# Last layer of a two-layer network: MLP, router and expert bias as fp16 halves inside the expert loop

## What is computed

```
# end of the attention-like block, per token
x  = x + o @ Wo
h2 = layernorm(x) * ln_w + ln_b
x  = x + gelu(h2 @ W1 + b1) @ W2 + b2          # "MLP": 128 -> 256 -> 128
# mixture of experts, all 16 experts on all tokens
x_ = layernorm(x)
logits = x_ @ router_w + router_b              # 16 experts
probs  = softmax(logits); top 4, renormalised -> c[token, expert], 0 elsewhere
for e in range(16):
    acc += (gelu(x_ @ w1[e] + b1[e]) @ w2[e] + b2[e]) * c[:, e]     # 128 -> 256 -> 128
out = x + acc
```

## Times and profile before

| | |
|---|---|
| time, median of 3 runs | 1009.13 us (1007.19 to 1015.8) |
| profiled execution, its own time | 1008.39 us |
| its span on the core | 1006.6 us |
| mean granted TensorE clock over the span | 0.919 |
| expert loop, 8 tiles | 619.1 to 1006.6 us |
| PE busy, whole span | 798.5 us |
| DVE busy, whole span | 678.7 us |
| ACT busy, whole span | 621.2 us |
| POOL busy, whole span | 630.4 us |

### The profile page before, as it was taken

The page is one execution under the profiler, slowest core; times in us unless marked ns, Lnnn a source line. Parts: engine busy times, 40 slices in busy tenths (PEclk is TensorE's granted clock), DMA queues, the critical chain, the costliest instruction groups (busy, mean ns, idle before and its releaser), DMA issues.

```text
span 1006.6 us, 17882 instructions
## 1 busy us (share of the span) xinstructions
PE 798.5 (79%) x5918; PEld 479.8 (48%) x5918; DVE 678.7 (67%) x1994; ACT 621.2 (62%) x923; POOL 630.4 (63%) x414
## 2 busy tenths in 40 slices
PE   1976465579777629828767688999999999999997
PEld 0443122125323125613222255777777777777776
DVE  5669899965554357749499776866665656666564
ACT  1755133314332327616967837989898888889895
POOL 4008799610545553646588895777777777777685
PEclk9977899978978858969999987999999999999999
DMA  5899200017000020043150000000000000000000
GB/s 132 99 121 204 91 0 0 17 31 204 31 12 7 4 72 25 23 125 96 45 175 1 0 1 1 2 11 0 10 0 10 0 11 0 10 0 10 0 12 12
DMA packets 52694, 40.42 MB, mean 40 GB/s; under 512 B 5995, under 2 KB 44638, under 8 KB 52638
## 3 DMA queue, kind: packets, MB, share of 16 engines
q1 hardware_dynamic: 49566, 37.27, 17.4%
q0 software_dynamic: 3072, 2.51, 0.9%
HBM read 18.05 MB, written 14.88 MB: 33 GB/s over the span
## 4 chain that ended last, share of the span: by engine, by line
PE 55%; DVE 11%; issue 4%; ACT 3%; another core or an unknown queue 3%; DMA 1%; POOL 1%; DVEq 0%; SPq 0%; POOLq 0%; ACTq 0%
PE PS L1684 53%; DVE scratch L1476 3%; DVE scratch L1484 2%; DVE resid L1413 2%; PE PS L1691 2%; ACT scratch L808 1%; DVE stats L1253 1%; POOL disp L600 1%; DVE scratch L1433 0%; DMA A<-disp 0%; PE PS L2080 0%; DVE scratch L1496 0%; DMA A<-y_rows 0%; DMA disp<-A,scratch 0%
## 5 line engine op out<-in xcount | busy, mean ns | idle before, releaser
L686 POOL TENSOR_TENSOR scratch<-scratch 128x1024 f16<-128x1024 f32 x128 | 272.8, 2133 | 105.2 <-ACT scratch L1065 102.3
L1637 DVE SCALAR_TENSOR_TENSOR resid<-PS,coef,resid 128x128 f32<-128x128 f32 x512 | 144.1, 344 | 135.8 <-PE PS L1684 134.0
L1684 PE MATMUL PS<-A,scratch 128*128 128x128 f16 x3456 | 217.4, 219 | 7.4 <-DVE A L1380 5.2
L1684 PEld LDWEIGHTS PS<-A,scratch 128*128 128x128 f16 x3456 | 204.0, 98 | 40.1 <-DVE A L1380 6.5
L1684 PE MATMUL PS<-A 128*128 (+1 forms) x768 | 188.2, 382 | 0.0
L1061 ACT ACTIVATE scratch<-PS,cols 128x512 f32<-128x512 f32 x256 | 164.0, 684 | 15.6 <-PE PS L1684 14.9
L1065 ACT ACTIVATE scratch<-scratch 128x1024 f16<-128x1024 f32 x128 | 135.3, 1057 | 5.2
L1684 PE MATMUL PS<-scratch,ident 128*128 128x512 f32 x160 | 89.5, 683 | 57.8 <-DVE scratch L1220 56.1
L563 POOL TENSOR_TENSOR scratch<-A 128x1024 f32<-128x1024 f32 x32 | 76.0, 2386 | 84.8 <-DVE A L1194 65.6
L600 POOL DMA_INDIRECT disp<-A,scratch x64 | 65.2, 1018 | 70.1 <-DVE scratch L1316 53.1
L1684 PEld LDWEIGHTS PS<-A 128*128 128x128 f16 x768 | 72.4, 99 | 72.0 <-issue 10.4
(11 more groups left out here) (295 smaller groups left out, 1345.9 us busy)
## 6 DMA issues: line engine op xcount, KB each, us to landing
A<-A SPq DMA_DIRECT2D x22, 256.0 KB, 8.4
y_rows<-zeros SPq DMA_DIRECT2D x8, 512.0 KB, 6.0
A<-y_rows SPq DMA_DIRECT2D x16, 256.0 KB, 3.6
disp<-zeros SPq DMA_DIRECT2D x4, 528.0 KB, 21.7
A<-disp SPq DMA_DIRECT2D x4, 528.0 KB, 5.9
resid<-in_L_attn_x SPq DMA_DIRECT2D x8, 256.0 KB, 4.5
A<-scratch SPq DMA_DIRECT2D x8, 256.0 KB, 7.9
A<-in_L_ffn_ew SPq DMA_DIRECT2D x1, 2048.0 KB, 12.9
```

Source lines behind the costliest of these rows:

```text
L686: pool.tensor_tensor(h_low[n % 4], h_full[n % 2], h_high[n % 4], SUB).then_inc(S("m1_low"), 1)
L1637: last = STT(out=resid[:, g, :], in0=bank(4 + e % 2)[:, t * C:(t + 1) * C], scalar=coef[:, t, e:e + 1], in1=resid[:, g, :], op0=MUL, op1=ADD)
L1684: return nc.tensor.matmul(o, l, r, start=start, stop=stop)
```

## The change

Four products of the side work are now made from fp16 halves: hidden layer and output of the MLP, the router's logits, and the bias times coefficients. For that:

- At the end of the first layer's expert stage ScalarE and VectorE make the halves of W1, W2 and the router's weights, of the identity and of the bias (in three copies, for which there are two more loads).
- VectorE makes the low half of the MLP's input (`hT11_low`, from PSUM), and both halves of the hidden layer (`hid11_split`: a cast and a subtraction for each of two parts). The normalisation's bias moves out of `hT11_copy` into the MLP's bias, with two tiny matmuls early in the program.
- The router takes the halves in `x_hl` that the experts use, so that ScalarE's copy into `xT12` is gone.
- The coefficients are written to one of two buffers; the copy L1674 is gone, and three operations write their scaled halves (`coef_parts`). The transposes of the coefficients are fp16 matmuls by an fp16 identity.
- For experts 5, 8 and 11 (`HIGH_BY_DVE`) VectorE makes `h_high` in place of ScalarE.
- Places: `outputs11` moves from behind e = 5 to behind 6, `add_mlp`, `inverse_deviation` and `normalise12` each one expert later (7, 8, 9), `normalise11` in all tiles to behind 10. `transpose12` stays behind 10.

```diff
-        A_(h_high[e % 4], h_full[e % 2], ACT.Copy).then_inc(S("m1_high"), 1)
+        if e not in HIGH_BY_DVE:
+            A_(h_high[e % 4], h_full[e % 2], ACT.Copy).then_inc(S("m1_high"), 1)
...
+            def hT11_low(c):
+                dve.wait_ge(S("xT_copied"), 3 * B + at(c))
+                STT(out=hT11_hl[:, 1, :], in0=bank(6), scalar=cols[:, LNW1:LNW1 + 1], in1=hT11_hl[:, 0, :], op0=MUL,
+                    op1=SUB).then_inc(S("xT_low"), 1)
+
+            def hid11_split(c, h):
+                dve.wait_ge(S("hid11"), at(2 * c + h))
+                st.done(V.tensor_copy(hid11_high[:, h, :], hid11[:, h, :]))
+                TT(hid11_low[:, h, :], hid11[:, h, :], hid11_high[:, h, :], SUB).then_inc(S("hid11_low"), 1)
+
+            def expert_high(b, e):
+                n = b * E1 + e
+                dve.wait_ge(S("m1_hid"), at(n * HC1 + HC1 - 1))
+                dve.wait_ge(S("m1_out_mm"), at(n, 4))
+                V.tensor_copy(h_high[e % 4], h_full[e % 2]).then_inc(S("eo"), 1)
...
-                st.done(TT(coef_next, weight, over(share_P), MUL))
+                to = coef[c % 2]
+                st.done(TT(to, weight, over(share_P), MUL))
+                high, low, again = (coef_parts[:, :, k * E1:(k + 1) * E1] for k in range(3))
+                TS(again, to, SCALE, None, MUL)
+                st.done(TS(high, to, SCALE, None, MUL))
+                st.done(STT(out=low, in0=to, scalar=SCALE, in1=high, op0=MUL, op1=SUB))
...
             def all_experts(b, next_batch, batch_beyond):
                 for e in range(E1):
+                    if e + 2 in HIGH_BY_DVE:
+                        expert_high(b, e + 2)
                     accumulate(b, e)
...
                     if next_batch:
-                        if e == 6:
+                        if e == 1:
+                            hT11_low(b + 1)
+                        if e == 3:
+                            hid11_split(b + 1, 0)
+                        if e == 5:
+                            hid11_split(b + 1, 1)
+                        if e == 7:
                             add_mlp(b + 1)
...
-                mm(bank(6), tile(u_1, h), hT11).then_inc(S("hid11_mm"), 1)
+                for k, (sw, sx) in enumerate(PARTS):
+                    last = mm(bank(6), tile(u1_hl[:, sw, :], h), hT11_hl[:, sx, :], start=k == 0, stop=k == len(PARTS) - 1)
+                last.then_inc(S("hid11_mm"), 1)
...
-                        if e == 5:
+                        if e == 6:
                             outputs11(b + 1)
```

More of the change, by code:

```diff
@@ L310, in build, with high_made @@
         prob, weight = (sm[:, 128 + 64 * k:192 + 64 * k].rearrange("p (n e) -> p n e", e=E1) for k in range(2))
-        coef_next, coef = coef1[:, 0:NT, :], coef1[:, NT:2 * NT, :]
+        coef = [coef1[:, NT * k:NT * k + NT, :] for k in range(2)]
         P7 = bank(7)
         share_P = P7[:, 4:8]
+        HIGH_BY_DVE = (5, 8, 11)
+        def high_made(b, e):
+            by_dve = sum(k <= e for k in HIGH_BY_DVE)
+            if e in HIGH_BY_DVE:
+                return S("eo"), E0 * NT + at(len(HIGH_BY_DVE) * b + by_dve - 1)
+            return S("m1_high"), at((E1 - len(HIGH_BY_DVE)) * b + e - by_dve)
         half_var_P, u_P, rx_P, rz_P = P7[:, 320:352], P7[:, 352:384], P7[:, 384:388], P7[:, 416:416 + TILES]
@@ L421, in _ @@
             load(u_r[:, :], I["L1_ffn_router_w"])
-            load(mb2[:, :], I["L1_ffn_b2"])
+            for k in range(3):
+                load(mb2[k * E1:(k + 1) * E1, :], I["L1_ffn_b2"])
             assert count == W_LOADS
@@ L742, in _ @@
             A_(u_gk, bank(2)[:, 0:64], ACT.Copy)
+            for h in range(2):
+                A_(cols[:, AB1 + h:AB1 + h + 1], bank(2)[:, 64 + h:65 + h], ACT.Identity, bias=cols[:, AB1 + h:AB1 + h + 1])
             def squares(src, dst, part):
@@ L1628, in _ @@
             route_weights(0)
-            st.done(V.tensor_copy(coef, coef_next))
             def accumulate(b, e):
@@ L1648, in all_experts @@
                         inverse_deviation(mv_z[:, 2 * NT:, 1], r_z[:, 2 * NT:], rz_P[:, 2 * NT:])
-                    if batch_beyond and e == (9 if b else 10):
+                    if batch_beyond and e == 10:
                         normalise11(b + 2)
                     if next_batch:
-                        if e == 6:
+                        if e == 1:
[5 more added lines that the diff above has]
+                        if e == 7:
                             add_mlp(b + 1)
-                        if e == 7:
+                        if e == 8:
                             inverse_deviation(mv_x[:, :, 1], r_x, rx_P)
-                        if e == 8:
+                        if e == 9:
                             normalise12(b + 1)
@@ L1737, in _ @@
             pe.wait_ge(s_cols, 2)
-            mm(bank(2)[:, 0:64], gk1T, u_gk2[:, :]).then_inc(s_colsT, 1)
+            mm(bank(2)[:, 0:64], gk1T, u_gk2[:, :])
+            for h in range(2):
+                last = mm(bank(2)[:, 64 + h:65 + h], tile(u_1, h), cols[:, LNB1:LNB1 + 1])
+            last.then_inc(s_colsT, 1)
             def square_sums(part):
@@ L2018, in logits12 @@
             def logits12(c):
-                pe.wait_ge(S("xs12"), at(c))
                 pe.wait_ge(S("x_low"), at(c))
                 for t in range(NT):
-                    last = mm(bank(6)[:, t * E1:(t + 1) * E1], tile(xT12, t), u_r[:, :])
+                    for k, (sx, sw) in enumerate(PARTS):
+                        last = mm(bank(6)[:, t * E1:(t + 1) * E1], x_hl[:, bass.ds(c * (2 * T) + sx * T + t * 128, 128)],
+                                  ur_hl[:, sw, :], start=k == 0, stop=k == len(PARTS) - 1)
                 last.then_inc(S("lg12_mm"), 1)
+            pe.wait_ge(S("split_low"), at(E0_SPLITS + 9))
             pe.wait_ge(s_nrm, 4)
@@ L2079, in coefficients_transposed @@
                 for t in range(NT):
-                    last = nc.tensor.transpose(tile(bank(6)[0:E1, :], t), coef[:, t, :], ident[:, :])
+                    last = mm(tile(bank(6)[0:3 * E1, :], t), coef_parts[:, t, :], ident16)
                 last.then_inc(S("m1_cT_mm"), 1)
```

85 lines of the change are left out of this document (54 added, 31 removed).

## The result

The change makes the kernel slower. The median is 1039.04 us after (1037.13 to 1042.59) and 1012.14 before, over four runs of each on one chip: 1.0257 times the time before, with a 95% interval of 1.022 to 1.0294. That is 26.9 us more; the forecast was 19.9 more and 1028, with a range from 1004 to 1040, so the measured median lies 1 us inside its upper end.

The account below looks back on a forecast made before the run. TensorE was taken to bound the kernel, busy 49.20 of 49.20 us per tile. Ahead of the loop 3.5, tile 0 5.9, six tiles 9.9 and the last 0.6 made 19.9 us more than 1008.39: 1028, range 1004 to 1040.

Parts of the forecast that it names:

- main case: Whole kernel: TensorE waits 1.7 us at each tile start, giving 1028 us, own range 1023 to 1033; chance 0.32.
- Start of a tile: Outputs of expert 2: TensorE waits 1.7 us for VectorE's sum of expert 0, behind the three coefficient operations.
- all three wait: Rival: every coefficient operation waits for GpSimd, so TensorE waits 3.0 us per tile start; 1037 us, chance 0.22.
- Hidden layer's low half: Hidden layer's input, behind VectorE's sum of expert 1: TensorE waits 0.45 us more.
- Middle: Hidden layer's splits at experts 3 and 5: VectorE done 0.3 us after TensorE wants the second, range 0 to 2.
- VectorE's casts above 0.69: Sign expected in the profile: VectorE's casts take longer than 0.69 us, the time assumed for 1024 elements.
- Transposes at expert 10: VectorE's chain from the end of expert 7 takes 9.3 us against TensorE's 7.9; TensorE waits 1.5 us.
- What TensorE gains: Side work in fp16 halves: 2.3 us less in each of seven tiles, 1.1 in the last, 17 if all else hides.
- Tile 0: Loop's first tile, with VectorE's statistics: TensorE waits 0.9, 3.5 and 3.8, together 8.2 us; less 2.3 gained, +5.9.
- Ahead of the loop: Stretch before the last layer's loop, where VectorE sets the pace: +3.5 us, range 0.5 to 6.
- The halves of the weights: End of the layer before: 1.7 us on VectorE, hidden in its 7.93 us wait for a DMA; cost nothing.
- Last tile: Loop's last tile: a wait of 1.7 us less a TensorE gain of 1.1, so +0.6.

Follow-up runs that it names:

- the router kernel: Changed kernel with the MLP back in fp32 and no VectorE casts of high halves, its three coefficient operations reading SBUF: 1020.37 us, ratio 1.0068.
- the router kernels: Changed kernel with MLP back in fp32: coefficient operations from PSUM (1000.09 us), from SBUF (1020.37), or from PSUM with VectorE's casts for experts 5, 8, 11 (1007.3).
- both cures: Changed kernel with coefficient operations reading PSUM and the router's transposes moved from behind expert 10 to behind expert 11: 1016.98 us, ratio 1.0071.

## Why the prediction was right, and where its sum was short

The side, the range and the mechanism held: VectorE, not TensorE, sets the pace at the forecast places. The sum was short, and the time came out above the main case's own range (1023 to 1033). By medians it is 26.9 for 19.9; in the two profiled executions the parts that the change touches grew by 31.9, and 3.1 of that is hidden by the shorter part ahead of them. Point by point:

- **Start of a tile: the term that was mis-sized.** Taken: 1.7. Measured: 2.65 in six of seven tiles (tile 2: 736.17, where it would have started at 733.52; 2.48 of it shows as idle time), and 1.3 less in the other (tile 3). The step that failed is "the copy at L1674 got in between two GpSimd operations, so a second, equally small one right behind it may". The first got in at the end of a GpSimd operation, exactly as that copy; in five of seven tiles the second found the next GpSimd operation already running, and so did the third. That was the rival *all three wait*: it put the wait at 3.0, since it had the third end at 6.0 after the transposes (in tile 1 it is 5.7), and it gave 52 us per tile where 51.87 came. That it gave 1037 where 1039 came is partly luck, since it too had nothing for the clock, below. L1180's 7.05 us had been the better row to follow: three operations in a row without a way in between. Twice the second did slip through: in tile 3, which is the case that I took for the usual one, and in the last tile, where no additions follow and the third waited for a whole low half:

```profile
782.24 1.90 DVE L1652 TENSOR_SCALAR coef<-coef 128x64 f16<-128x64 f32 x1
784.05 0.18 DVE L1653 TENSOR_SCALAR coef<-coef 128x64 f16<-128x64 f32 x1
784.27 1.18 DVE L1654 SCALAR_TENSOR_TENSOR coef<-coef 128x64 f16<-128x64 f32 x1
...
991.44 0.18 DVE L1653 TENSOR_SCALAR coef<-coef 128x64 f16<-128x64 f32 x1
991.65 2.14 DVE L1654 SCALAR_TENSOR_TENSOR coef<-coef 128x64 f16<-128x64 f32 x1
```

  The rule of the Trainium skill that stood beside the rival ("SBUF — State Buffer", "SBUF: two separate sides") fits all three operations in five of seven starts. The Trainium skill limits the rule there to VectorE instructions in a two-port mode or with two inputs in SBUF; the run with PSUM operands (225 ns for 1903) agrees with that limit. It does not say why the second got through in two starts of seven, and in three of seven in the router kernel; that stays open.
- **Hidden layer's low half.** Taken 0.45, measured 0.54 (0.38 idle). Right.
- **Middle.** Taken 0.3, measured 0. But the 3.2 lost earlier in the tile cover it: with the first wait removed, 0.70 appears. The size was wrong, the place right. The sign "VectorE's casts above 0.69" hardly came: the 24 casts of high halves take a median of 0.693 (at most 1.07), since where they stand GpSimd is mostly waiting for them (57.9 us in all).
- **Transposes at expert 10.** Taken 1.5, measured 1.53 (763.31 less 761.78). The sum itself gave 9.3 less 7.9, that is 1.4; as it ran, from the end of expert 7 on TensorE (753.88), it is 9.43 less 7.90. The chain, timeline of VectorE and GpSimd in tile 2, with the pieces that were added up from the earlier trace rows:

```profile
755.12 0.68 DVE L1603 SCALAR_TENSOR_TENSOR resid<-PS,resid 128x512 f32<-128x512 f32 x1
...
760.40 0.69 DVE L1597 CAST scratch<-scratch 128x1024 f16<-128x1024 f32 x1
761.01 1.12 DVE L1696 SCALAR_TENSOR_TENSOR resid<-PS,coef,resid 128x128 f32<-128x128 f32 x4
762.05 1.11 DVE L1572 SCALAR_TENSOR_TENSOR scratch<-resid,scratch,PS 128x128 f32<-128x128 f32 x4
...
761.18 4.22 POOL L707 TENSOR_TENSOR scratch<-scratch 128x1024 f16<-128x1024 f32 x2 [3.85 <-DVE scratch L1597]
```

  In tile 0 it was 3.8 by forecast and 3.81 in the profile. A chain added up from measured pieces came out to some 0.1, because no GpSimd operation held one of them there: the cast, the one piece of a waiting kind, ran while GpSimd stood idle for it (3.85). The cast of 0.69, bounded between 0.42 and 0.84, took 0.69.
- **What TensorE gains.** Taken 2.3 per tile, measured 2.05 (4.72 of waits less the 2.67 that the tile grew). Up to the transposes at expert 10, where the hidden layer's two parts stand, the gain is 1.02 (29.44 = 34.16 less 4.72 of waits, against 30.46 with the fp32 MLP), as taken; behind them it is 1.03 (17.71 against 18.74) for 1.28. The transposed coefficients and the bias take 0.33 and 0.32 where 0.22 each was taken; the logits 0.57 where 0.67 was. So a piece of four matmuls cost more here (0.32 to 0.33) than four times the share of one in a row of 24 (0.22). The rest of the difference was not followed up.
- **Tile 0.** Taken +5.9, measured +6.8 (56.04 against 49.28). Within it TensorE is idle 0.51 for 0.9 at the hidden layer, 2.40 for 3.5 at its output, 3.81 for 3.8 at the transposes. Behind the transposes the clock fell, which was not in the sum: from there to the next tile it takes 19.39 instead of the 17.71 of tile 2, 1.7 more. Without that the tile would have come out below the forecast.
- **Ahead of the loop.** Taken 3.5, measured 3.9. In the router kernels it is 37.6 to 38.6, in those with the MLP's halves 42.9 to 43.5: it is the MLP's halves that cost it, and TensorE's longest wait there, 5.03, is for their split, as argued. The halves of the weights, taken at nothing, are made on VectorE from 435.47 to 437.10 in after, ahead of 4.72 us in which it waits for a DMA: nothing.
- **Last tile.** Taken +0.6, measured +3.8 (46.8 from 988.56 to the end, before 43.0 from 963.60): the wait 0.9 longer than taken, 1.5 of clock, 0.3 less gain, and 0.5 behind TensorE's last matmuls, which was not followed up.
- **The sum, again with what was measured.** 3.9 + 6.8 + 6 x 2.67 + 3.8, + 2.7 for the clock in tiles 1 and 6, - 1.3 for tile 3, in which the second operation slipped through = 31.9. It is 12.0 over the forecast: 6.1 from the six tiles (0.95 of wait and 0.25 of gain in each, less what the middle didn't cost), 3.2 from the last, 2.7 and -1.3 as above, 0.4 ahead of the loop and 0.9 in tile 0. The clock, in all 5.8 of it in four tiles (1.7, 1.3, 1.3 and 1.5), was a cost that the forecast did not have at all, and about as large as what the waits of the coefficient operations were short by.

What the parts of the change are worth, by the loop in the profiles: router and bias -7.3 if their operands are in PSUM (380.2 against 387.5), but +11.8 as they are written (399.3). The MLP's halves and casts added on top of the good form: +20.2 as placed (400.4 against 380.2), of which 9.4 go when the transposes move one expert later (391.0), and 3.6 more without tile 0's statistics (387.4). About 5 more stand ahead of the loop. TensorE does gain the 1.0 us per tile from them that was added up, but VectorE has its 5 us of work in places where TensorE waits for it. None of the versions with the MLP's halves beat before. An arrangement that hides them was not found, and was not searched for beyond these.

## What to carry to other kernels

Here a tiny VectorE instruction with only SBUF operands, placed where GpSimd ran back to back, took as long as GpSimd's running instruction (1.90 instead of 0.2 us), and each further one behind it mostly took another (1.30, 1.34): count such instructions, not their elements, and try an operand in PSUM if there is room (225 ns here). Before giving work to an engine that has slack on average, add up its chain ahead of each deadline from measured pieces; where no GpSimd instruction held the pieces, that sum came out to about 0.1 us here (9.43 for 9.3). A wait can also cost more than itself, through the clock. And measure the parts of a change apart: here one part was worth 1.2%, and it was hidden by another part and by where three operands lay.

## What the runs showed of the hardware that was not expected

**The clock of TensorE after a stall.** A wait of 2.5 us can cost more than itself. Granted clock of after by stretch, behind the wait of 3.81 in tile 0 and the waits of 2.44 to 2.49 in tiles 1, 6 and 7 (the columns are those of the stretches above):

```profile
656.00:660.00 4.00, 3.44 (x13) 1.73 (x14) 2.48 (x10) 1.90 (x4) 2.31 (x2) 0.61 0.03 6
...
684.00:688.00 4.00, 3.77 (x18) 1.56 (x16) 1.79 (x6) 1.65 (x3) 1.75 (x1) 0.57 0.00 0
...
944.00:948.00 4.00, 3.76 (x19) 1.68 (x19) 1.55 (x6) 2.25 (x4) 1.15 (x1) 0.62 0.00 0
...
996.00:1000.00 4.00, 4.00 (x39) 3.09 (x37) 1.91 (x6) 1.18 (x2) 0.40 (x2) 0.72 0.02 4
```

0.57 of full speed is near the lower of the two levels (1.2 of 2.4 GHz). Tiles 1 and 6, in which it fell, took 53.20 and 53.21, those with the same waits and a clock of 1.00 took 51.87: 1.3 us each. In the last tile the first 24 small matmuls after the wait take 2.72 instead of 1.50. The kernel with router and bias from SBUF shows the same 2.72 at 930.00, and the same kernel from PSUM, which has no such waits, a clock of 1.00 in the stretches shown. Until TensorE's work at the end is done, no fall inside the loop in any of these ten profiles came without a wait ahead of it, and the shortest such wait was 2.00 (no cast on VectorE, 809.04). But it happened after three of the six waits of 2.44 to 2.49 us in after, and after one of 2.61 in the kernel with both cures it did not; what tells these apart was not found.

**Fewer instructions on VectorE, more waiting.** Without the three casts the second subtraction of 512 elements took 2.50 us instead of 0.69 in every tile, since the pause of 2.02 us in which GpSimd waited for a cast was no longer there. The two engines set each other's starts here, both through semaphores and through the waiting of SBUF operands, and the one that was relieved of work became later.
